# Reordering steps in a two-layer transformer kernel on one core: four-bit lines, key split, normalised rows, second normalisation

## Chip, core and metric

One NeuronCore of one Trainium2 chip runs the whole program in one launch. The metric is the device time of that launch in microseconds (us); lower is better. Engines are named as the profile names them: PE (TensorE, matrix products and transposes), ACT (ScalarE), DVE (VectorE), POOL (GpSimd), SP (the queue that issues the DMAs).

## The reference, cut to what matters

Four sequences of 256 tokens, width 512, pass through two pre-normalised layers. Each layer is an attention and a feed-forward part, both added to the residual stream.

```python
x = L0_attn_q                                   # (4, 256, 512) float32
x = x + attn0(layernorm(x))    # 32 heads in 8 groups, causal, softmax, output projection
x = x + lora(layernorm(x))     # 64 experts of rank 16, the 16 best by score, softmax gates
x = x + attn1(layernorm(x))    # q and k RMS-normalised, ALiBi slopes, softmax, projection
x = x + ffn(layernorm(x))      # gate, up and down weights in four-bit NF4 codes x absmax
```

A four-bit weight is `NF4_CODE[q] * absmax` of its block of 64. It has to be unpacked before it is multiplied.

## The kernel before

**Precision.** Every product is float32 made of three fp32r products: each operand is split into a high and a low part, and a matmul is `lo*hi + hi*lo + hi*hi` (lines 312 to 314). So each operand has a split: on the way out of PSUM the high part is an ACT copy (`pt_hi`, `ot_hi`, `qt_hi`, `kt_hi`, `xt_hi`) and the low part a DVE subtraction (`pt_lo`, `ot_lo`, `qt_lo`, `kt_lo`, `xt_lo`). Weights that come by DMA, and the second layer's keys, are split by POOL (`split_steps`, lines 570 and 571).

**Slots.** An attention layer walks over 8 groups of heads, and in each over 4 batches. One pair (group g, batch b) is a slot. Seven turns of a hardware loop hold slots b = 1, 2, 3 of group g and slot 0 of group g+1 (`slot_steps`); before them stand lead steps and a first slot, behind them the last three slots of the last group (`last_slot_steps`) and a tail (`tail_steps`). What a slot does is written out as one list of steps. PE, ACT, DVE, POOL and SP each walk the same list in order, each issuing only its own share of a step and waiting on semaphores for the others. Where a step stands in the list therefore sets its place in every engine's queue.

The steps of a slot that matter here:

- `pt_split`: three transposed probability tiles of the slot before leave PSUM, `pt_hi` on ACT (L804), `pt_lo` on DVE (L862).
- `scores`, `mask`, `max`, `exp`, `normalise`: the softmax of this slot. PE makes the scores; DVE masks, takes the maximum and its bias; ACT takes the exponential (L813); DVE divides (L900). Part 0 are the first 128 queries, part 1 the second 128 with all 256 keys.
- `tile`: one of six 512-wide projections (K, Q0 to Q3, V) for a half of the tokens, made ahead for later slots. The main results go alternately to two PSUM banks (`ring`); a bank is free again when DVE has taken the low part out of it.
- `pv`: probabilities times values on PE, then `ot_hi` (ACT) and `ot_lo` (DVE). PE waits here for all three `pt_lo`.
- `out`: the output projection of 128 tokens, added to x by DVE (L911).
- `transpose`: the normalised probabilities, part 0 (L784), then part 1 (L791).
- `dq_lines` (ACT, four or eight ACTIVATE, L546), `dq_top` (DVE, L553 and L555) and `dq_value` (POOL, L561, L562, then `centre` L537 for the next codes): one tile of four-bit weights unpacked in each slot of the first attention, written to HBM for the last part. `dq_lines` waits until `centre` is done.
- second layer only: `q_rms`, `k_rms`, `roots` and `k_norm`. In `k_norm` PE spreads the key's root (L777), DVE multiplies the keys by it (L967), and POOL copies and splits them (L1019, L570, L571); the scores of the slot after need that split. `w_next` is the refill of one weight tile: SP loads it and POOL splits it (2 instructions).

**The layer norm.** `norm_stats` (DVE) takes mean and variance of a batch of x, `norm_root` takes the inverse root (14 small instructions on POOL, or on DVE), `norm_write` writes the normed rows into `xn` (ACT, L473, or DVE, L419) and `norm_turn` transposes them (PE, L460) and splits them into `xt_hi` and `xt_lo`. `xn` holds one batch, so the next write has to wait for the transposes of the last. ACT's `norm_write` also waits until DVE has freed every ring tile that ACT has counted up to there. In the last slots a batch is normed as soon as its x is complete, so that the next part can begin.

**Around the attentions.** Behind the first attention stand the experts, which begin with the scores of batch 0. Behind the second stands the four-bit part. It works in units of one 512-wide gate and up product (`unit`), `silu`, `h`, then `down`; its first list of steps is `opening`, and `lines`, `top`, `value` there are the unpacking of the `late` weights.

Of the kernel before, what the change touches and what calls it, by code (L numbers as in the profile page):

```python
# [34 lines left out]
GROUPS, HEADS = 8, 4  # L35
# [11 lines left out]
K, Q0, Q1, Q2, Q3, V = range(6)  # L47
# [50 lines left out]
def slot_steps(b, rms):  # L98


    if rms:
        half, ahead = (0 if b in (1, 2) else 1), (0 if b == 0 else 1)
        tiles = [K, Q0, Q1] if b in (1, 3) else [Q2, Q3, V]
    else:
        half, ahead = (1, 0) if b in (0, 1) else (0, 1)
        tiles = [K, Q0, Q1] if b in (0, 2) else [Q2, Q3, V]
    t = [("tile", x, half, ahead) for x in tiles]
    roots = rms and b in (1, 3)
    s = [("pt_split",)] + ([] if rms or b == 1 else [("dq_lines", 0)])
    s += [("scores", 0), ("mask", 0), ("max", 0, 0)]  # L110
    s += t[0:1] + [("max", 1, 0)] if rms else [("max", 1, 0)] + t[0:1]
    s += [("exp", 0), ("normalise", 0)] + t[1:2]
    s += [] if rms else [("exp", 1)]
    s += [("q_rms_turn", 1 if b == 1 else 0)] if roots else []
    s += [("pv",)] + ([("exp", 1)] if rms else [("dq_lines", 0)] if b == 1 else [])
    s += [("roots", 1 if b == 1 else 0)] if roots else []
    s += [("k_rms", half)] if rms and tiles[0] == K else []
    s += [("roots_done",)] if roots else []
    s += t[2:3] + [("normalise", 1)] + ([] if rms else [("dq_lines", 1), ("dq_top", 0)]) + [("out", 0)]
    s += [("v_turn", half)] if tiles[-1] == V else []  # L120
    s += [("w_next", X) for X in (Q0, Q1)] if rms and b == 3 else []
    s += [("k_norm", 1 if b == 1 else 0)] if roots else []
    s += [] if rms else [("dq_top", 1)]
    if rms:
        s += [("out", 1), ("q_rms", half, 0 if tiles[0] == K else 1)]
    else:
        s += [("out", 1), ("dq_value",)] if b == 0 else [("dq_value",), ("out", 1)]
    return s + [("transpose",)]


def first_slot_steps(rms):


    softmax = [[("scores", 0), ("mask", 0), ("max", 0, 0)], [("max", 1, 0), ("exp", 0), ("normalise", 0)], [("exp", 1)]]
    if rms:
        s = [("q_rms", 1, 0), ("tile", Q2, 1, 0)] + softmax[0] + [("w_next", K)] + softmax[1] + [("tile", Q3, 1, 0)]
        s += [("w_next", Q0)] + softmax[2] + [("tile", V, 1, 0), ("q_rms", 1, 1), ("w_next", Q1), ("v_turn", 1)]
        return s + [("normalise", 1)] + [("w_next", X) for X in (Q2, Q3, V)] + [("transpose",)]
    s = softmax[0] + [("tile", K, 1, 0)] + softmax[1] + [("tile", Q0, 1, 0)] + softmax[2] + [("tile", Q1, 1, 0)]
    return s + [("normalise", 1), ("dq_first",), ("transpose",)]  # L140


def last_slot_steps(b, rms):


    if b == 1 and not rms:
        return [step for step in slot_steps(1, rms) if step[0][0:3] != "dq_"][:-1] + [("scores", 1), ("transpose",)]
    s = [("pt_split",)] + ([("norm_turn", 0)] if b == 3 else []) + ([("scores", 0)] if b == 1 else [])
    if rms and b == 1:
        s += [("q_rms_turn", 1), ("pv",), ("mask", 0)]  # L150
    else:
        s += [("mask", 0), ("pv",)]
    s += [("max", 0, 0), ("exp", 0), ("max", 1, 0)] + ([("roots", 1)] if rms and b == 1 else [])
    s += norm_begin([b - 2], "pool") if b >= 2 else []
    s += [("normalise", 0), ("exp", 1), ("normalise", 1), ("out", 0)]
    s += [("k_norm", 1)] if rms and b == 1 else []
    if rms and b in (1, 2):
        s += [("ffn_hi", k) for k in (2 * b - 2, 2 * b - 1)] + [("ffn_lo", k) for k in (2 * b - 2, 2 * b - 1)]
    s += [("norm_write", b - 2, "act")] if b >= 2 else []
    s += [("out", 1)] + ([("scores", 1)] if b < 3 else [])  # L160
    return s + [("transpose",)]


def norm_begin(batches, who):


    s = [("norm_stats", batches), ("norm_root", batches, who)]
    return s + ([("norm_write", batches[0], "dve")] if who == "dve" else [])
# [15 lines left out]
    return s + [("tile", x, 0, 0) for x in (Q1, Q2, Q3, V)] + [("v_turn", 0)]  # L184


def tail_steps():

    return [("pt_split",), ("norm_turn", 1), ("pv",)] + norm_begin([2], "pool") + [("norm_write", 2, "act"), ("out", 0), ("out", 1),
                                                                 ("norm_turn", 2)]  # L190


RING_STEPS = ("tile", "k_rms", "v_turn", "q_rms", "q_rms_turn", "k_norm", "out")
# [51 lines left out]
def build(nc, x_in, w_attn, w_dense, lora_a, lora_wr, lora_b, norm_w, codes, absmax, kept, out):  # L245

    with ExitStack() as ctx:
# [3 lines left out]
        def sb(name, shape, dt=F32, scope=ctx):  # L251
            return scope.enter_context(nc.sbuf_tensor(name, shape, dt))
# [322 lines left out]
        def attention(layer, scope):  # L575
            rms = layer == 1
# [484 lines left out]
            def walk(eng, do, grows, pool_like=False):  # L1061


                xn_lead[0] = p1[:, :, :].rearrange("p h k -> p (h k)").rearrange("p (t d) -> p t d", d=D) if rms else None
                do(eng, lead_steps(rms), 0, None)
                xn_lead[0] = None
                lead2[0] = True
                do(eng, first_slot_steps(rms), 0, 0)
                lead2[0] = False
                last = GROUPS - 1  # L1070

                def turn(g, **more):
                    for b in (1, 2, 3):
                        do(eng, slot_steps(b, rms), g, b, **more)
                    do(eng, slot_steps(0, rms), g + 1, 0, **more)

                if pool_like:
                    turn_loop(eng, last - 1, grows, turn)
                    turn(last - 1, refill=not rms, final=True)
                else:  # L1080
                    turn_loop(eng, last, grows, turn)
                if do is pe_steps:
                    last_slots[layer] = pe_ring.n
                for b in (1, 2, 3):
                    do(eng, last_slot_steps(b, rms), last, b)
                do(eng, tail_steps(), GROUPS, 0)


            hi_turn = 2 * (WT - 1 - rms) + 2
# [404 lines left out]
        def nf4(scope):  # L1494
# [3 lines left out]
            h_hi = sb("h_hi", [P, 2, TOK], F32R, scope)  # L1498
            h_lo = sb("h_lo", [P, 2, TOK], F32R, scope)
# [10 lines left out]
            def tops(par, ahead):  # L1510
                return [("top", par, 0, ahead), ("top", par, 1, ahead), ("value", par, ahead)]
# [19 lines left out]
                return s + half_unit(3) + (splits(1, 2, 3) if more else []) + downs(more)  # L1531

            opening = [("centre", 0, 0), ("centre", 1, 0), ("unit", 0), ("lines", 0, 0, 0), ("lines", 0, 1, 0)]
            opening += norm_begin([3], "dve") + [("silu", 0), ("h", 0), ("h_hi", 0), ("norm_turn", 3), ("h_lo", 0)]
            opening += tops(0, 0) + [("unit", 1), ("lines", 1, 0, 0), ("silu", 1), ("top", 1, 0, 0), ("h", 1)]
            opening += [("h_hi", 1), ("lines", 1, 1, 0), ("h_lo", 1), ("top", 1, 1, 0), ("value", 1, 0)]
            opening += half_unit(2) + splits(0, 4, 5) + splits(1, 0, 1) + half_unit(3) + splits(1, 2, 3) + downs(True)
# [183 lines left out]
        with d_scope:  # L1721
            pe_d, act_d, dve_d, pool_d, sp_d = nf4(d_scope)
# [135 lines left out]
```

## Time and profile before

| | |
|---|---|
| median of 3 runs | 1869.03 us (1868.91 to 1872.07) |
| profiled execution | 1863.55 us |
| its span | 1861.8 us |
| PE busy | 1751.9 us, 94% |
| DVE busy | 1296.9 us, 70% |
| ACT busy | 877.7 us, 47% |
| POOL busy | 788.6 us, 42% |
| granted TensorE clock, mean | 0.981 |

The profiled execution is one run; its span is first instruction to last. The engines work side by side, so PE's 94% says that the other 110 us are the time in which PE waited. A busy figure alone does not say which wait can be removed; for that the waits of PE are read in their place. The parts lie in the span like this: first attention to about 710 us, experts to 840, second attention to 1610, four-bit part to the end. A turn of the first attention's loop takes some 84 us, one of the second some 90.

### The profile page before, as it was taken

How to read it: one execution, taken by the hardware profiler on the slowest of the kernel's cores; microseconds unless marked ns; L12 is line 12 of the kernel's file. 1: busy time of each engine (PE TensorE's matmuls, PEld its weight loads, DVE VectorE, ACT ScalarE, POOL GpSimd, SP SyncE). 2: the span in 40 equal slices, each digit the busy share in tenths (PEclk: the TensorE clock that was granted, in tenths of full speed). 3: DMA queues.
4: the chain of work that ended last, by engine and by line, in shares of the span. 5: the costliest groups of instructions: out<-in, count | busy, mean ns of one | idle time of the engine just before them, and what ended most of it. 6: DMA issues, size and time to landing. Idle time of an engine off the chain costs nothing.

```text
span 1861.8 us, 28756 instructions
## 1 busy us (share of the span) xinstructions
PE 1751.9 (94%) x8864; PEld 1449.6 (78%) x8864; DVE 1296.9 (70%) x2317; ACT 877.7 (47%) x2288; POOL 788.6 (42%) x924
## 2 busy tenths in 40 slices
PE   8999999999999977997899999999999997889999
PEld 7787878788787866885778787878787886668887
DVE  5787778777788765345677777877777776655555
ACT  3556565556555634222444444444444444454543
POOL 5334425262534433144545454545454424244442
PEclk9999999999999998999899999999999999999999
DMA  4022122121112121000101000000001002022121
GB/s 143 33 68 73 60 64 90 43 95 65 62 62 77 47 71 57 1 7 23 35 29 28 28 29 28 28 28 28 28 28 28 23 0 80 0 69 68 56 56 46
DMA packets 47711, 87.77 MB, mean 47 GB/s; under 512 B 6576, under 2 KB 6576, under 8 KB 47536
## 3 DMA queue, kind: packets, MB, share of 16 engines
q1 hardware_dynamic: 47664, 87.19, 14.8%
q8 instruction: 24, 0.39, 0.1%
q14 instruction: 23, 0.19, 0.0%
HBM read 77.73 MB, written 9.44 MB: 47 GB/s over the span
## 4 chain that ended last, share of the span: by engine, by line
PE 54%; DVE 6%; POOL 4%; ACT 3%; issue 2%; POOLq 0%; DVEq 0%; ACTq 0%
PE ring L312 10%; PE ring L314 9%; PE ring L313 9%; PE scores L312 3%; PE scores L314 3%; PE scores L313 3%; PE turned L312 3%; PE turned L313 3%; PE turned L314 3%; PE scores L705 2%; PE turned L791 1%; PE turned L755 1%; PE turned L756 1%; PE turned L777 1%; PE turned L784 1%
## 5 line engine op out<-in xcount | busy, mean ns | idle before, releaser
L312 PE MATMUL ring<-xt_hi,w_lo 128*128 128x512 f32 x768 | 306.3, 399 | 18.9 <-DVE kt_lo L930 14.9
L313 PE MATMUL ring<-xt_lo,w_hi 128*128 128x512 f32 x768 | 304.7, 397 | 0.0
L314 PE MATMUL ring<-xt_hi,w_hi 128*128 128x512 f32 x768 | 304.5, 397 | 0.0
L312 PE MATMUL ring<-wd_hi,ot_lo 128*128 128x512 f32 x512 | 208.3, 407 | 8.2 <-DVE ot_lo L906 6.4
L804 ACT CAST pt_hi<-turned 128x512 fp32r<-128x512 f32 x192 | 100.6, 590 | 237.7 <-PE turned L784 231.0
L313 PE MATMUL ring<-wd_lo,ot_hi 128*128 128x512 f32 x512 | 203.7, 398 | 0.0
L314 PE MATMUL ring<-wd_hi,ot_hi 128*128 128x512 f32 x512 | 203.6, 398 | 0.0
L312 PEld LDWEIGHTS ring<-xt_hi,w_lo 128*128 128x128 f32 x768 | 145.6, 190 | 53.9 <-issue 19.1
L570 POOL TENSOR_SCALAR sq_hi<-sq 128x512 fp32r<-128x512 f32 x80 | 55.0, 687 | 305.4 <-ACT sq L830 286.9
L314 PEld LDWEIGHTS ring<-xt_hi,w_hi 128*128 128x128 f32 x768 | 145.3, 189 | 34.9
L546 ACT ACTIVATE lv_early<-code_early 128x512 f32<-128x512 f32 x224 | 122.6, 631 | 102.9 <-POOL code_early L537 95.0
L313 PEld LDWEIGHTS ring<-xt_lo,w_hi 128*128 128x128 f32 x768 | 145.7, 190 | 31.4
L900 DVE TENSOR_TENSOR p<-p,rsum 128x512 f32<-128x512 f32 (+1 forms) x128 | 150.1, 1173 | 4.4
L862 DVE TENSOR_TENSOR pt_lo<-turned,pt_hi 128x512 fp32r<-128x512 f32 x192 | 120.8, 683 | 35.9 <-ACT pt_hi L804 35.9
L830 ACT ACTIVATE sq<-ring 128x512 f32<-128x512 f32 x80 | 48.3, 604 | 191.6 <-PE ring L314 183.5
L813 ACT ACTIVATE p<-scores,bias,root 128x128 f32<-128x128 f32 (+1 forms) x256 | 128.0, 519 | 19.0 <-DVE bias L890 19.0
L561 POOL TENSOR_TENSOR deq_early<-lv_early 128x512 f32<-128x512 f32 x28 | 37.9, 1354 | 228.8 <-DVE lv_early L555 196.9
L571 POOL TENSOR_TENSOR w_lo<-w_raw,w_hi 128x512 fp32r<-128x512 f32 x96 | 130.2, 1356 | 8.0
L930 DVE TENSOR_TENSOR qt_lo<-ring,qt_hi 128x512 fp32r<-128x512 f32 x128 | 88.1, 688 | 61.7 <-ACT qt_hi L840 60.3
L911 DVE TENSOR_TENSOR x<-x,ring 128x512 f32<-128x512 f32 x128 | 87.0, 682 | 53.4 <-PE ring L314 52.8
L570 POOL TENSOR_SCALAR w_hi<-w_raw 128x512 fp32r<-128x512 f32 x96 | 77.0, 802 | 110.9 <-DMA w_raw<-w_attn_dram 57.4
L906 DVE TENSOR_TENSOR ot_lo<-turned,ot_hi 128x512 fp32r<-128x512 f32 x128 | 83.5, 685 | 57.7 <-ACT ot_hi L819 57.6
(247 smaller groups left out, 4480.6 us busy)
## 6 DMA issues: line engine op xcount, KB each, us to landing
w_raw<-w_attn_dram SPq DMA_DIRECT2D x96, 256.0 KB, 3.1
wd_raw<-w_dense_dram SPq DMA_DIRECT2D x64, 256.0 KB, 2.7
code_early<-codes_dram SPq DMA_DIRECT2D x28, 256.0 KB, 2.8
absmax_early<-absmax_dram SPq DMA_DIRECT2D x56, 128.0 KB, 3.0
kept_dram<-deq_early SPq DMA_DIRECT2D x28, 256.0 KB, 2.0
stage<-kept_dram SPq DMA_DIRECT2D x28, 256.0 KB, 2.7
code_late<-codes_dram SPq DMA_DIRECT2D x14, 256.0 KB, 2.7
absmax_late<-absmax_dram SPq DMA_DIRECT2D x28, 128.0 KB, 2.9
```

Of the source, the lines that this page charges most:

```text
L312: nc.tensor.matmul(o, l_lo, r_hi, start=start, stop=False)
L313: nc.tensor.matmul(o, l_hi, r_lo, start=False, stop=False)
L314: return nc.tensor.matmul(o, l_hi, r_hi, start=False, stop=stop)
L546: ins = nc.scalar.activation(lv[:, q, :], code[:, par, :], ACT.Copy, bias=offset, scale=scale)
L570: pool_link(nc.gpsimd.tensor_scalar(dst_hi, src, 1.0, 0.0, ALU.mult, ALU.add))
L571: nc.gpsimd.tensor_tensor(dst_lo, src, as_f32(dst_hi), ALU.subtract).then_inc(sem_done, 1)
L804: nc.scalar.copy(pt_hi[:, j, :, :], turned[:, j, :, :]).then_inc(s_pt_hi, 1)
L813: ins = nc.scalar.activation(pr[:, h, :], sc[:, h, :], ACT.Exp, bias=bias[:, k, h:h + 1], scale=scale, accum_out=sums[:, k, h:h + 1])
L862: nc.vector.tensor_tensor(pt_lo[:, j, :, :], turned[:, j, :, :], as_f32(pt_hi[:, j, :, :]), ALU.subtract).then_inc(s_pt_lo, 1)
L900: nc.vector.tensor_tensor(pr[:, :, :], pr[:, :, :], rsum[:, k, :].unsqueeze(2).to_broadcast([P, HEADS, width]), ALU.mult).then_inc(s_prob, 1)
L911: dve_ring_free(nc.vector.tensor_tensor(x[:, t, :], x[:, t, :], tile, ALU.add))
L930: dve_ring_free(nc.vector.tensor_tensor(lo, tile, as_f32(hi), ALU.subtract))
```

## The change

It moves steps in the lists and removes no work.

1. Third slot (b = 2) of the first attention: `dq_lines 0` (4 ACTIVATE) moves from behind `pt_split` to behind `pv`, where the second slot has it already.
2. Fourth slot (b = 3) of the second attention: `k_norm` moves ahead of the refills of Q0 and Q1.
3. First slots. First attention: `exp 0` and `exp 1` come ahead of Q0's tile step, `max 1` ahead of K's, and `normalise 1` ahead of Q1's. Second: `normalise 1` moves ahead of `q_rms`.
4. Last slots and tail: the `norm_write` of a batch moves from its slot's end to behind the next slot's `pt_split`, and its `norm_turn` from ahead of `pv` to behind it. In the second slot of the second attention `k_norm` moves behind the second `out`.
5. The last attention's tail leaves `norm_turn 2` to the four-bit part, where it stands behind the first unit and the root of batch 3.

```diff
@@ slot_steps
-    s = [("pt_split",)] + ([] if rms or b == 1 else [("dq_lines", 0)])
+    s = [("pt_split",)] + ([] if rms or b in (1, 2) else [("dq_lines", 0)])
...
-    s += [("pv",)] + ([("exp", 1)] if rms else [("dq_lines", 0)] if b == 1 else [])
+    s += [("pv",)] + ([("exp", 1)] if rms else [("dq_lines", 0)] if b in (1, 2) else [])
...
+    s += [("k_norm", 1 if b == 1 else 0)] if roots else []
     s += [("w_next", X) for X in (Q0, Q1)] if rms and b == 3 else []
-    s += [("k_norm", 1 if b == 1 else 0)] if roots else []
@@ first_slot_steps
-        s += [("w_next", Q0)] + softmax[2] + [("tile", V, 1, 0), ("q_rms", 1, 1), ("w_next", Q1), ("v_turn", 1)]
-        return s + [("normalise", 1)] + [("w_next", X) for X in (Q2, Q3, V)] + [("transpose",)]
-    s = softmax[0] + [("tile", K, 1, 0)] + softmax[1] + [("tile", Q0, 1, 0)] + softmax[2] + [("tile", Q1, 1, 0)]
-    return s + [("normalise", 1), ("dq_first",), ("transpose",)]
+        s += [("w_next", Q0)] + softmax[2] + [("tile", V, 1, 0), ("normalise", 1), ("q_rms", 1, 1), ("w_next", Q1)]
+        return s + [("v_turn", 1)] + [("w_next", X) for X in (Q2, Q3, V)] + [("transpose",)]
+    s = softmax[0] + softmax[1][0:1] + [("tile", K, 1, 0)] + softmax[1][1:] + softmax[2] + [("tile", Q0, 1, 0)]
+    return s + [("normalise", 1), ("tile", Q1, 1, 0), ("dq_first",), ("transpose",)]
@@ last_slot_steps
-    s = [("pt_split",)] + ([("norm_turn", 0)] if b == 3 else []) + ([("scores", 0)] if b == 1 else [])
+    s = [("pt_split",)] + ([("norm_write", 0, "act")] if b == 3 else []) + ([("scores", 0)] if b == 1 else [])
...
-        s += [("mask", 0), ("pv",)]
+        s += [("mask", 0), ("pv",)] + ([("norm_turn", 0)] if b == 3 else [])
...
-    s += [("k_norm", 1)] if rms and b == 1 else []
     if rms and b in (1, 2):
         s += [("ffn_hi", k) for k in (2 * b - 2, 2 * b - 1)] + [("ffn_lo", k) for k in (2 * b - 2, 2 * b - 1)]
-    s += [("norm_write", b - 2, "act")] if b >= 2 else []
-    s += [("out", 1)] + ([("scores", 1)] if b < 3 else [])
+    s += [("out", 1)] + ([("k_norm", 1)] if rms and b == 1 else []) + ([("scores", 1)] if b < 3 else [])
@@ tail_steps
-    return [("pt_split",), ("norm_turn", 1), ("pv",)] + norm_begin([2], "pool") + [("norm_write", 2, "act"), ("out", 0), ("out", 1),
-                                                                 ("norm_turn", 2)]
+    s = [("pt_split",), ("norm_write", 1, "act"), ("pv",), ("norm_turn", 1)] + norm_begin([2], "pool")
+    s += [("out", 0), ("out", 1), ("norm_write", 2, "act")]
+    return s + ([] if rms else [("norm_turn", 2)])
@@ nf4, opening
-            opening += norm_begin([3], "dve") + [("silu", 0), ("h", 0), ("h_hi", 0), ("norm_turn", 3), ("h_lo", 0)]
+            opening += [("norm_stats", [3]), ("norm_root", [3], "dve"), ("norm_turn", 2), ("norm_write", 3, "dve")]
+            opening += [("silu", 0), ("h", 0), ("h_hi", 0), ("norm_turn", 3), ("h_lo", 0)]
```

## Rows read from the trace of the kernel before

**Rows 1.** The page: PE's line, and PE's clock in 40 slices (tenths).

```profile
PE 1751.9 (94%) x8864; PEld 1449.6 (78%) x8864; DVE 1296.9 (70%) x2317; ACT 877.7 (47%) x2288; POOL 788.6 (42%) x924
...
PEclk9999999999999998999899999999999999999999
```

**Rows 2.** Waits of PE: us in total, times, longest us.

```profile
PE ring L312 <- DVE kt_lo L930: 14.9, 6, 2.7
PE ring L460 <- ACT xn L473: 14.9, 7, 3.5
PE scores L705 <- POOL kt_lo L571: 10.7, 7, 1.7
```

**Rows 3.** Windows: three third slots; length, busy of PE, PEld, DVE, ACT, POOL, clock.

```profile
74.13:93.85 19.72, 19.72 (x103) 16.47 (x101) 15.88 (x26) 12.41 (x35) 3.22 (x3) 1.00 0.12 41
153.73:177.86 24.13, 20.18 (x103) 16.38 (x101) 16.65 (x25) 12.31 (x35) 9.72 (x9) 1.00 0.12 36
237.75:261.69 23.94, 21.62 (x102) 17.54 (x101) 17.16 (x25) 12.41 (x35) 9.54 (x9) 0.93 0.13 39
```

**Rows 4.** Timeline of the second of these: start, us, engine, [idle before, releaser].

```profile
163.90 2.19 ACT L546 ACTIVATE lv_early<-code_early 128x512 f32<-128x512 f32 x4 [7.97 <-POOL code_early L537]
167.68 0.49 PE L312 MATMUL ring<-xt_hi,w_lo 128*128 128x512 f32 x1 [2.52 <-DVE kt_lo L930]
172.17 0.48 PE L312 MATMUL ring<-wd_hi,ot_lo 128*128 128x512 f32 x1 [1.43 <-DVE ot_lo L906]
```

**Rows 5.** Timeline of a fourth slot's end, second attention.

```profile
1058.08 1.87 DVE L900 TENSOR_TENSOR p<-p,rsum 128x1024 f32<-128x1024 f32 x1
1058.84 1.59 POOL L570 TENSOR_SCALAR w_hi<-w_raw 128x512 fp32r<-128x512 f32 x1
1060.47 0.67 DVE L967 TENSOR_TENSOR k_raw<-k_raw,turned 128x512 f32<-128x512 f32 x1
1063.73 0.40 POOL L1019 TENSOR_SCALAR kt_f<-k_raw 128x256 f32<-128x256 f32 x1
1066.12 1.16 PE L705 MATMUL scores<-kt_f,qt_f 128*128 128x128 f32 x8 [1.71 <-POOL kt_lo L571]
```

**Rows 6.** Timelines of the two first slots.

```profile
49.20 0.69 DVE L930 TENSOR_TENSOR qt_lo<-ring,qt_hi 128x512 fp32r<-128x512 f32 x1 [1.78 <-ACT qt_hi L840]
51.56 1.75 PE L791 MATMUL turned<-ident,p 128*128 128x128 f32 x7 [2.86 <-DVE p L900]
904.69 1.54 PE L791 MATMUL turned<-ident,p 128*128 128x128 f32 x6 [2.49 <-DVE p L900]
```

**Rows 7.** Timeline of the first attention's last slots and tail.

```profile
663.11 0.50 PE L312 MATMUL turned<-pt_hi,v_lo 128*128 128x512 f32 x1 [1.72 <-DVE pt_lo L862]
676.26 1.52 ACT L473 ACTIVATE xn<-x,shift,rstd 128x512 f32<-128x512 f32 x2 [5.28 <-POOL shift L448]
677.21 1.33 PE L460 MATMUL ring<-ident,xn 128*128 128x128 f32 x8 [2.10 <-ACT xn L473]
680.22 0.80 PE L312 MATMUL turned<-pt_hi,v_lo 128*128 128x512 f32 x1 [1.67 <-DVE pt_lo L862]
715.11 0.45 PE L312 MATMUL ring<-xt_hi,a_lo 128*64 128x256 f32 x1 [2.34 <-DVE xt_lo L490]
```

**Rows 8.** Timeline from the second attention's last slots to the four-bit part.

```profile
1551.63 1.13 PE L777 MATMUL turned<-ident,root 128*128 128x128 f32 x8 [4.08 <-DVE q_slope L960]
1557.62 1.13 PE L705 MATMUL scores<-kt_f,qt_f 128*128 128x128 f32 x8 [0.52 <-POOL kt_lo L571]
1634.25 0.50 PE L312 MATMUL scores<-xt_hi,w_lo 128*128 128x512 f32 x1 [3.78 <-DVE hf L1655]
```

**Rows 9.** Windows: three stretches in the last slots; columns as in rows 3.

```profile
678.80:685.70 6.90, 5.48 (x13) 4.34 (x14) 5.07 (x10) 2.56 (x5) 0.00 (x0) 0.51 0.00 0
695.90:702.80 6.90, 5.57 (x17) 4.43 (x18) 3.77 (x6) 3.83 (x8) 0.00 (x0) 0.51 0.00 0
1552.70:1556.10 3.40, 3.40 (x10) 2.62 (x9) 2.27 (x3) 0.04 (x1) 0.97 (x2) 0.50 0.00 0
```

More of the change, by code:

```diff
@@ L184, in lead_steps, with tail_steps @@
     return s + [("tile", x, 0, 0) for x in (Q1, Q2, Q3, V)] + [("v_turn", 0)]
-def tail_steps():
-    return [("pt_split",), ("norm_turn", 1), ("pv",)] + norm_begin([2], "pool") + [("norm_write", 2, "act"), ("out", 0), ("out", 1),
-                                                                 ("norm_turn", 2)]
+def tail_steps(rms):
+    s = [("pt_split",), ("norm_write", 1, "act"), ("pv",), ("norm_turn", 1)] + norm_begin([2], "pool")
+    s += [("out", 0), ("out", 1), ("norm_write", 2, "act")]
+    return s + ([] if rms else [("norm_turn", 2)])
 RING_STEPS = ("tile", "k_rms", "v_turn", "q_rms", "q_rms_turn", "k_norm", "out")
@@ L1085, in walk @@
                     do(eng, last_slot_steps(b, rms), last, b)
-                do(eng, tail_steps(), GROUPS, 0)
+                do(eng, tail_steps(rms), GROUPS, 0)
             hi_turn = 2 * (WT - 1 - rms) + 2
```

## The prediction

> **What bounds the kernel now.** I read the page first: PE is busy for 1751.9 of the 1861.8 us, so 110 us are waits of PE, and the clock line has dips to 0.8 and 0.9 [rows 1]. No other engine is near that share, so the time is PE's work, plus its waits, plus what a low clock adds. Next I read PE's waits in total [rows 2], then each wait's place on the timeline. The reader is to see that they are few and regular. The kt_lo wait comes in six of the seven third slots of the first attention's loop. The kt_lo wait of POOL is once per turn of the second loop in six turns, 1.7 each, and once at 1557.62 with 0.52 [rows 2, 8]. Of the seven xn waits three stand in each attention's last slots and tail (14.2 us together) and one in the experts. Last I read the windows for the clock, because a wait can be followed by a stretch at 0.50, which is 1.2 of the 2.4 GHz [rows 9].
>
> **Part 1, the four-bit lines in the third slot.** The lines of the third slot wait for POOL's `centre`, which here is done 10.2 us after the slot begins. ACT stands idle for 7.97 us with the copies of K, both exponentials and ot_hi queued behind it. So kt_lo is late and PE waits 2.52 us for its bank, and then 1.43 us for ot_lo [rows 4]. In the first turn `centre` is early, nothing waits, and the slot takes 19.72 us of PE work. In the turn after it takes 24.13, and in the next 23.94, with one wait and a clock of 0.93 instead of the second wait [rows 3]. So a late `centre` costs 4.2 to 4.4 us per turn, whether as wait or as clock.
> Behind `pv` the 4 ACTIVATE come when ACT has made both exponentials and ot_hi. K is ready some 6.5 us into the slot as in the first turn, and by the durations of this slot (two copies, exp 0, two copies, exp 1, two ot_hi) ACT reaches the lines some 13 us in, about 3 us after `centre` is done; that chain of POOL hangs on the output weights of an earlier slot and not on this slot's pace. The lines take 2.19 [rows 4] and then stand ahead of Q1's copies, which end 1.5 us after Q1 is ready; normalise 1 follows at some 18 us, and the transposes need it at 20. So the slot should fall to 19.7 to 20.1. The tops and the x adds end 2 to 3 us behind the transposes, as they do in the first turn, and their next reader is a pv four tiles later. Bounds: the kt_lo waits alone go (6 x 2.5 = 15), or all to the floor (6 x 4.35 = 26). I take 24.5.
>
> **Part 2, key split ahead of two refills.** DVE's multiply of the keys ends at 1061.14, POOL is then in the refills and begins the key's copies at 1063.73; they last 2.3 us, and PE, idle since 1064.41, starts the scores at 1066.12 [rows 5]. With the split first it runs 1061.2 to 1063.5, 0.9 us before PE wants it. The whole 1.71 goes in six turns: 10.2. The two refills, some 4 us, come 2.4 us later; POOL's next work is the squares of the slot after, 8 us behind, and SP's loads that wait for these refills are wanted more than 10 us later. If the split were held up by another 1.9 us (the length of the longest DVE instruction near it, L900), 1.0 of each wait would stay and the part were worth 4.2; that is the lower bound.
> The rows show such a hold: the refill's first instruction took 1.59 beside a 1.87 us DVE instruction with two SBUF inputs [rows 5]. The Trainium skill (SBUF — State Buffer, Who interferes with whom) says that a DVE instruction with two SBUF inputs contends with a GpSimd instruction that reads SBUF, and that the later one fully blocks. By that rule the split's new neighbours (adds with one input from PSUM) do not hold it and the part is worth 10.2; if any DVE neighbour did, it would be 4.2. The trace cannot yet say which, since no row has the split there.
>
> **Part 3, the first slots.** In the first attention DVE waits 1.78 us for ACT's qt_hi before Q1's subtraction, and normalise 1 is queued behind it; PE waits 2.86 for that [rows 6]. Now normalise 1 stands behind Q0's subtraction instead. The exponentials come 1.3 us earlier but Q0's copies now stand between, so I get normalise 1 some 1.2 us earlier, and the clock may stay up (up to 3.4 more): 1.2 to 4.6, I take 2.5. In the second, normalise 1 waits behind q_rms and v_turn though its exponentials are done 5 us before; PE's 2.49 [rows 6] goes but v_turn comes 0.5 later: 2.0 to 3.7, I take 2.5. Sum 5, bounds 3 and 8.
>
> **Part 4, last slots and tail.** Transposes end at 675.11 (677.21 less 2.10). ACT then waits for POOL's root until 676.26 and writes two xn (1.52) before it copies pt_hi, so pv starts at 680.22. In the slot before, with nothing in between, pv waits 1.72 behind the transposes [rows 7]. So after the change it starts at 675.11 + 1.72 = 676.83, 3.4 earlier. norm_turn (1.33) now comes behind pv, and its two xt_lo delay the maxima by 1.3: the next transposes come 3.3 earlier, not more. In the tail the same happens, longer, since POOL's root ends later there; pv comes some 4.4 earlier again. The root of batch 2 and its turn follow pv as before, so that wait stays, and so does 2.34 for the experts' first product [rows 7]. Together 7.8, of which some 4.8 is work that the old slots did at a clock of 0.51 [rows 9]; if one such stretch remains it is 1 to 2 less. Bounds 3 and 8.5, I take 7.
> In the second attention the same two turns give 2.4 and 3.4, and norm_turn 2 behind the first unit takes its xn wait off PE; but the four-bit part then goes by ACT and DVE (lines, xt_hi, write 3, h), which the wait of 3.78 at 1634.25 shows [rows 8]. Following that chain, it comes 6.3 earlier in all.
> Against this stands `k_norm` behind the second out. PE's wait of 4.08 for the roots [rows 8] is partly filled by the out (3.0 us), but the scores behind hang on roots, key multiply and POOL's split, and DVE's multiply now follows one more add of 0.7. They start 0.6 later, at 1558.2, and PE idles 5.7 us before them with 1 us of small work. After 4.08 idle the clock was 0.50 for 3.4 us [rows 9]; after more idle I expect the same under the scores, half of 3.4 = 1.7. With another dip elsewhere in these slots (1.0), the second attention's end gives 6.3 - 0.6 - 1.7 - 1.0 = 3.0, bounds -2 and 6.
>
> **The sum.** 24.5 + 10.2 + 5 + 7 + 3.0 = 49.7 us off the profiled execution's 1863.55 (span 1861.8): 1813.9. That execution is 5.5 us under the median of the runs shown, 1869.03; the gain is the same from there, so I predict 1819.3. The bounds give 15 + 4.2 + 3 + 3 - 2 = 23 and 26 + 10.2 + 8 + 8.5 + 6 = 59: 1846 and 1810, and 5.5 less if the runs should fall where the profiled one did.
>
> **Rivals.**
> A. *The third slot gives back half.* ACT or DVE becomes the slot's bound: lines, Q1's copies, normalise 1 and the tops all queue at its end. DVE is busy for 16.65 of 24.13 [rows 3], which would be 84% of a slot of 19.8. For it: the order there has only 2 us of slack. Against: the second slot has this order already and runs without a wait. Part 1 is 12 and the time 1832.
> B. *The ends give nothing.* Waits only change their names: pv waits for pt_lo, the scores for the kt split, and the clock stays low. For it: every one of those chains is longer than PE's work there. Then 10 less: 1829.
> C. *Slower.* `centre` in the third slot slips past the point where ACT gets to the lines. From 3 us later than now it stops ACT ahead of Q1's copies and the second lines, and every further us is one us in each of six turns. To eat 49.7 us it must come 3 + 8.3 = 11 us later than now: say 12, which gives 1874. Against: POOL does the same work in the same order, and `centre` has stood at the same place in the turns that I read.
> D. *It does not do what it says.* Waits of PE are replaced one for one because PE's own queue was not waiting for what the profile names: 1869.
>
> **How the numbers follow.** My forecast 0.74, A 0.11, B 0.09, C 0.03, D 0.03. The range 1806 to 1838 takes in the forecast with its bounds, A and B, and leaves out C and D and the far ends. A change of 0.2% (3.7 us) is about what a measurement of this kernel tells from none. Faster by more than that: 0.94 (forecast, A, B). Within it: D, 0.03. Slower: C, 0.03.
>
> **What the changed profile would show.** Part 1: no kt_lo wait at L312, ACT's idle time before lv_early gone from the third slots, and these slots at 19.7 to 20.1; a wait of L784 for p or of L312 for qt_lo in them speaks for A. Part 2: no wait of L705 in the second loop, and the key split ahead of two w splits. Part 3: L791's waits at 1.7 and near 0. Part 4: two xn waits fewer in the first attention; pt_lo waits of 1.7 to 2.2 in their place; the first unit some 10 us earlier but its second half only 6; and a wait of some 5 us of L705 behind the second out of the second attention's last group, then a clock of 0.50. I should be wrong above all if the slots shorten and new waits of the same size show on ot_lo or p in the slot behind.

## The result, and the profile after

The changed kernel takes 1815.65 us (median of 4 runs, 1813.52 to 1816.80) against 1868.97 for the kernel before (1867.81 to 1872.07). The ratio is 0.9711, with a 95% interval of 0.9694 to 0.9728: 53 us or 2.9% faster. Forecast were 1819.3 us. The profiled execution took 1815.49 us with a span of 1813.8.

The page: PE's line and its clock in 40 slices. They answer to [rows 1].

```profile
PE 1739.9 (96%) x8864; PEld 1445.1 (80%) x8864; DVE 1299.4 (72%) x2317; ACT 877.6 (48%) x2288; POOL 786.2 (43%) x924
...
PEclk9999999999999998999999999999999999999999
```

No work has gone: each engine has as many instructions in this line as before. PE's busy time is 12 us less and its idle time fell from 110 to 74 us; together that is the 48 us. The mean granted clock rose from 0.981 to 0.986; an estimate from the two means (the missing share times the span, 35 and 25 us) puts some 10 of the 12 us down to it. (The lines of the changed kernel stand one lower than before: L312 is L311 here.)

PE's waits, in total. They answer to [rows 2].

```profile
PE turned L311 <- DVE pt_lo L861: 10.7, 6, 1.9
PE ring L311 <- DVE xt_lo L489: 9.2, 8, 2.3
PE scores L704 <- POOL kt_lo L570: 6.4, 1, 6.4
PE turned L754 <- POOL sq_lo L570: 5.4, 2, 2.9
```

The six kt_lo waits of DVE are gone from the list. POOL's kt_lo was waited for seven times with 10.7 us, and is now waited for once, but for 6.4. The waits for xt_lo are partly new: the turned rows stand behind pv and the output product behind them.

Windows of the changed kernel: the third slots of the first two turns, then the fourth slot behind the second of them. Columns as in [rows 3].

```profile
69.81:89.47 19.66, 19.66 (x102) 16.52 (x101) 15.02 (x24) 12.42 (x35) 3.22 (x3) 1.00 0.12 41
149.86:169.51 19.65, 19.65 (x102) 16.52 (x101) 15.30 (x23) 12.43 (x35) 10.07 (x9) 1.00 0.15 47
169.51:190.13 20.62, 20.33 (x106) 16.86 (x105) 17.44 (x28) 12.25 (x34) 3.22 (x3) 1.00 0.11 38
```

The second third slot took 24.13 [rows 3] and now takes as long as that of the first turn. The fourth slot has 0.29 of idle time in it. It is part of a price of 0.5 that the slot behind pays (20.62 against 20.11 before), and experiment 5 takes it away. ACT's first instructions on the four-bit lines of that slot, in the kernel before and in the changed one:

```profile
182.48 2.19 ACT L546 ACTIVATE lv_early<-code_early 128x512 f32<-128x512 f32 x4 [2.42 <-POOL code_early L537]
...
175.74 2.20 ACT L545 ACTIVATE lv_early<-code_early 128x512 f32<-128x512 f32 x4 [4.02 <-POOL code_early L536]
```

The slot begins at 177.86 and 169.51: ACT gets to the lines 4.6 us into it before and 6.2 now, and Q2's copies and the exponentials stand behind.

Timeline of that third slot in the changed kernel, to be read against [rows 4].

```profile
156.49 0.37 ACT L834 COPY kt_f<-ring 128x256 f32<-128x256 f32 x1 [4.42 <-PE ring L313]
...
159.40 0.94 POOL L536 TENSOR_SCALAR code_early<-code_early 128x512 f32<-128x512 int32 x1
...
162.79 2.25 ACT L545 ACTIVATE lv_early<-code_early 128x512 f32<-128x512 f32 x4
```

`centre` is as late in the slot as before (10.5 us in), but K's copies no longer wait for it, and ACT comes to the lines 2.45 us after it is done. The forecast had "about 3". `centre` itself took 0.94 us here instead of 0.62; it ran beside DVE's `normalise`, which took 0.86 instead of 0.69.

Timeline of a fourth slot's end in the second attention, against [rows 5].

```profile
1025.86 0.67 DVE L966 TENSOR_TENSOR k_raw<-k_raw,turned 128x512 f32<-128x512 f32 x1
...
1026.69 0.41 POOL L1018 TENSOR_SCALAR kt_f<-k_raw 128x256 f32<-128x256 f32 x1 [2.44 <-DVE k_raw L966]
...
1027.77 1.28 POOL L570 TENSOR_TENSOR kt_lo<-k_raw,kt_hi 128x512 fp32r<-128x512 f32 x1
...
1029.02 0.61 POOL L569 TENSOR_SCALAR w_hi<-w_raw 128x512 fp32r<-128x512 f32 x1
...
1029.64 1.06 PE L704 MATMUL scores<-kt_f,qt_f 128*128 128x128 f32 x8
```

The split now ends at 1029.05, 0.6 before PE wants it, the scores have no wait, and the refills follow. The split takes 2.36 us from its first copy to its end, against 2.33 before: nothing held it.

Where the 48.1 us between the two profiled spans came from can be read off matching transposes (the first of each slot) in both traces. The first slot of the first attention is 4.7 shorter, the loop and the slots up to the third of the last group 22.9, the last slots up to the experts' first product 8.7 (715.11 [rows 7] against 679.20). Then 6.8 are lost again up to the first transposes of the second attention. That slot is 3.6 shorter, the loop 11.6, and the way from the last group to the end gives 3.7; the start differs by 0.4. The sum is 4.7 + 22.9 + 8.7 - 6.8 + 3.6 + 11.6 + 3.7 - 0.4 = 48.0.

Of the 6.8 us lost, 0.7 belong to part 3. `normalise 1` now stands ahead of `q_rms` on DVE, so `v_turn`, just ahead of those transposes, comes later; PE waits 1.49 for it here and 0.77 with the old order. Timelines of the changed kernel and of undo_first (experiment 3):

```profile
871.09 1.11 PE L736 MATMUL turned<-ident,vt 128*128 128x128 f32 x4 [1.49 <-DVE xn L942]
...
869.62 1.11 PE L736 MATMUL turned<-ident,vt 128*128 128x128 f32 x4 [0.77 <-DVE xn L942]
```

### The profile page after: what moved, and what is told of

Same layout as the page of the kernel before. It is cut to its first block, busy times and chain, and to the rows that moved or that the text cites. A ratio compares the mean times of both kernels' runs of the same rounds, so it can differ in the third digit from the quotient of the medians.

```text
span 1813.8 us, 28744 instructions
## 1 busy us (share of the span) xinstructions
PE 1739.9 (96%) x8864; PEld 1445.1 (80%) x8864; DVE 1299.4 (72%) x2317; ACT 877.6 (48%) x2288; POOL 786.2 (43%) x924
## 4 chain that ended last, share of the span: by engine, by line
PE 55%; DVE 5%; ACT 3%; POOL 2%; issue 2%; DMA 0%; POOLq 0%; DVEq 0%; ACTq 0%; SPq 0%
PE ring L311 10%; PE ring L312 10%; PE ring L313 10%; PE scores L311 3%; PE scores L313 3%; PE scores L312 3%; PE turned L311 3%; PE turned L313 3%; PE turned L312 3%; PE scores L704 2%; PE turned L790 2%; PE turned L783 1%; PE turned L754 1%; PE turned L776 1%; PE turned L755 1%
## 5 line engine op out<-in xcount | busy, mean ns | idle before, releaser
L311 PE MATMUL ring<-xt_hi,w_lo 128*128 128x512 f32 x768 | 304.6, 397 | 3.9 <-DVE qt_lo L929 1.5
L312 PE MATMUL ring<-xt_lo,w_hi 128*128 128x512 f32 x768 | 303.8, 396 | 0.0
L311 PE MATMUL ring<-wd_hi,ot_lo 128*128 128x512 f32 x512 | 207.6, 405 | 9.8 <-DVE xt_lo L489 5.0
L312 PE MATMUL ring<-wd_lo,ot_hi 128*128 128x512 f32 x512 | 202.8, 396 | 0.0
L311 PEld LDWEIGHTS ring<-xt_hi,w_lo 128*128 128x128 f32 x768 | 145.1, 189 | 36.6 <-DVE qt_lo L929 2.0
L312 PEld LDWEIGHTS ring<-xt_lo,w_hi 128*128 128x128 f32 x768 | 144.9, 189 | 31.5
L899 DVE TENSOR_TENSOR p<-p,rsum 128x512 f32<-128x512 f32 (+1 forms) x128 | 154.2, 1205 | 4.4
L311 PEld LDWEIGHTS ring<-wd_hi,ot_lo 128*128 128x128 f32 x512 | 96.4, 188 | 36.2 <-issue 8.9
L887 DVE TENSOR_REDUCE negmax<-scores 128x4 f32<-128x512 f32 (+1 forms) x128 | 121.9, 953 | 2.1
```

Source lines behind the costliest of these rows:

```text
L311: nc.tensor.matmul(o, l_lo, r_hi, start=start, stop=False)
L312: nc.tensor.matmul(o, l_hi, r_lo, start=False, stop=False)
L887: dve_link(nc.vector.tensor_reduce(negmax[:, k, :], sc[:, :, :], AX.X, ALU.max, negate=True))
L899: nc.vector.tensor_tensor(pr[:, :, :], pr[:, :, :], rsum[:, k, :].unsqueeze(2).to_broadcast([P, HEADS, width]), ALU.mult).then_inc(s_prob, 1)
```

## Experiments

Each run was compared with the kernel before on the same chip (medians there 1869.4 to 1870.0). The differences in us below are taken from the changed kernel's 1815.65, which is of an earlier set of runs. Measured again beside key_back, lines_fourth and both, the changed kernel took 1812.88 (after_again). So a difference of 3 us or less between medians tells nothing by itself; there the traces decide, stage by stage.

| run | median us | ratio, 95% interval |
|---|---|---|
| undo_lines | 1837.86 | 0.9835 (0.9814 to 0.9856) |
| undo_key | 1826.35 | 0.9768 (0.9743 to 0.9792) |
| undo_first | 1825.17 | 0.9766 (0.9746 to 0.9787) |
| undo_rows | 1831.08 | 0.9798 (0.9775 to 0.9821) |
| key_back | 1811.87 | 0.9696 (0.9674 to 0.9718) |
| lines_fourth | 1811.48 | 0.9687 (0.9673 to 0.9700) |
| both | 1806.90 | 0.9678 (0.9656 to 0.9700) |
| after_again | 1812.88 | 0.9703 (0.9688 to 0.9718) |
| undo_turn2 | 1816.55 | 0.9731 (0.9706 to 0.9756) |
| late_centre1 | 1815.67 | 0.9723 (0.9703 to 0.9742) |
| late_centre4 | 1835.60 | 0.9831 (0.9812 to 0.9851) |

**1. undo_lines: part 1 undone.**

```diff
-    s = [("pt_split",)] + ([] if rms or b in (1, 2) else [("dq_lines", 0)])
+    s = [("pt_split",)] + ([] if rms or b == 1 else [("dq_lines", 0)])
-    s += ... [("dq_lines", 0)] if b in (1, 2) else [])
+    s += ... [("dq_lines", 0)] if b == 1 else [])
```

> The changed kernel with its first part undone: the four-bit lines of the third slot stand behind pt_split again. My theory: ACT waits for POOL's centre ahead of K's copies again, so the kt_lo waits of 2 to 2.7 us come back in six third slots. In the two traces so far these slots differ by 26.4 us, and 3.5 come back from the fourth slots, which are 0.5 longer in the changed kernel: the run should take 23 us more than the changed kernel, 1838.5, and its fourth slots should be 0.5 shorter. Rival: the third slot gained from what stands around it (a faster turn of POOL or DVE), and the lines alone are worth half or less: 1827 or under, with the waits back but elsewhere made good.

Measured: 1837.86, 22.2 more than the changed kernel's median. PE's waits in total, first line:

```profile
PE ring L311 <- DVE kt_lo L929: 14.8, 6, 2.7
```

The six waits are back with their old size (14.9 [rows 2]). The six third slots are 4.2 to 4.7 us longer, 26 in all, and the seven fourth slots 0.5 shorter. The theory holds; the rival asked for 1827 or less.

**2. undo_key: part 2 undone.**

```diff
-    s += [("k_norm", 1 if b == 1 else 0)] if roots else []
     s += [("w_next", X) for X in (Q0, Q1)] if rms and b == 3 else []
+    s += [("k_norm", 1 if b == 1 else 0)] if roots else []
```

> The changed kernel with its second part undone: k_norm stands behind the refills of Q0 and Q1 again. My theory: the wait of the scores for POOL's kt_lo, 1.7 us, comes back in six turns, and with it the restart that makes a turn 1.97 shorter in the changed trace: 11.6 us more, 1827. Rival: the split was held by DVE instructions with two SBUF inputs and its place hardly counts: 4 us more, 1820.

Measured: 1826.35, 10.7 more. The wait is back in six turns, which with the one of 6.4 makes 16.7:

```profile
PE scores L704 <- POOL kt_lo L570: 16.7, 7, 6.4
```

In the trace a turn is 1.98 us longer in five of the six and 3.5 in one, where a stretch at a clock of 0.50 came upon it.

**3. undo_first: part 3 undone.** Both first slots stand in the order before, as in the diff ahead of the prediction.

> The changed kernel with its third part undone: the first slots of both attentions in the old order. My theory: waits of 2.9 and 2.5 us for p come back, each with a stretch at a clock of 0.50: 4.7 and 3.6 by the two traces, 8 in all, 1824. Rival: the clock does not depend on these waits, and only the waits' own 1.9 and 2.5 come back: 4 us, 1820.

Measured: 1825.17, 9.5 more. Timeline of the first attention's first slot in this run:

```profile
51.68 1.97 PE L790 MATMUL turned<-ident,p 128*128 128x128 f32 x8 [2.86 <-DVE p L899]
```

Its window behind that wait (length, busy of PE, PEld, DVE, ACT, POOL, clock, DMA):

```profile
50.90:57.70 6.80, 6.02 (x28) 6.02 (x29) 2.71 (x4) 1.17 (x2) 1.20 (x1) 0.50 0.16 41
```

The same place in the changed kernel:

```profile
50.09 1.09 PE L790 MATMUL turned<-ident,p 128*128 128x128 f32 x8 [0.97 <-DVE p L899]
```

With the wait of 2.86 the clock falls to 0.50 and the eight transposes take 1.97; with one of 0.97 it stays up and they take 1.09. The slot's 4.7 us are 1.9 of wait; the other 2.8 are put down to the clock, as what is left. The second attention's first slot is 3.6 longer in this run, of which the 0.7 us of `v_turn` ahead of it are to be taken off. Both halves speak for the theory and against the rival.

**4. undo_rows: parts 4 and 5 undone, k_norm left behind the second out.** `norm_write` at the slot's end, `norm_turn` ahead of `pv`, the four-bit part's opening as before.

> The changed kernel with its fourth and fifth part undone but for k_norm, which stays behind the second out: xn is written ahead of the slot's end and turned ahead of pv, in both attentions, and the four-bit part opens as before. My theory: three xn waits come back in each attention's end; 8.7 us in the first attention and 7.2 in the second by the two traces (2.5 + 4.7), 16 in all, 1831.5. Rival: the pt_lo waits stand in for them and the gain of the ends is clock and chance: 8 us or less, 1823.

Measured: 1831.08, 15.4 more. The waits for xn are back (16.1, 7 times) and those for xt_lo fall from 9.2 to 4.1:

```profile
PE ring L459 <- ACT xn L472: 16.1, 7, 3.5
...
PE ring L311 <- DVE xt_lo L489: 4.1, 4, 2.3
```

So a part of the xn waits does live on under another name, but the ends give 15 us and not 8. The traces agree: from the first attention's third slot of the last group to the experts' first product 41.4 us pass instead of 32.8, and from the last group of the second attention to the end 329.2 instead of 321.9, 15.9 in all.

**5. lines_fourth: the lines behind pv in the fourth slot too.** This tests why that slot became longer.

```diff
-    s = [("pt_split",)] + ([] if rms or b in (1, 2) else [("dq_lines", 0)])
+    s = [("pt_split",)] + ([] if rms or b in (1, 2, 3) else [("dq_lines", 0)])
-    s += ... [("dq_lines", 0)] if b in (1, 2) else [])
+    s += ... [("dq_lines", 0)] if b in (1, 2, 3) else [])
```

> The changed kernel with the four-bit lines behind pv in the fourth slot too. My theory: the fourth slot is 0.5 us longer in the changed kernel because its centre is now later than the slot's pt_split, ACT waits for it and ot_hi, ot_lo and the output product come late by as much; with the lines behind pv that goes: 7 x 0.5 = 3.5 us less, 1812.1. Rival: the lines then delay the tops and x adds, and slot 0 of the next group pays the same: 1815.6 or more.

Measured: 1811.48, 4.2 under the changed kernel's first median and 1.4 under its second (1812.88). The window of that fourth slot, where the changed kernel needs 20.62:

```profile
169.07:189.18 20.11, 20.11 (x106) 16.96 (x105) 17.51 (x28) 12.23 (x34) 3.22 (x3) 1.00 0.12 39
```

All seven fourth slots are 0.5 shorter, to the length before, and slot 0 behind them is no longer. In the traces that is 3.5 us. The theory holds by the traces; the medians alone could not tell it from the rival.

**6. key_back: k_norm ahead of the second out again, in the last group's second slot of the second attention.**

```diff
     s += [("normalise", 0), ("exp", 1), ("normalise", 1), ("out", 0)]
+    s += [("k_norm", 1)] if rms and b == 1 else []
...
-    s += [("out", 1)] + ([("k_norm", 1)] if rms and b == 1 else []) + ([("scores", 1)] if b < 3 else [])
+    s += [("out", 1)] + ([("scores", 1)] if b < 3 else [])
```

> The changed kernel, but in the second slot of the second attention's last group k_norm stands ahead of the second out again, as before the change. My theory: that step of part 4 loses time, since the scores behind hang on roots, key multiply and POOL's split and not on PE. The wait of 6.4 us for kt_lo with its low clock goes back to 0.5, and the slot is 3.4 shorter: 1812.2. Rival: PE's wait of 4 us for the roots comes back and costs as much: 1815.6.

Measured: 1811.87, which is 3.8 under the first median of the changed kernel and 1.0 under its second. Timeline of this run, PE's wait for the roots:

```profile
1507.05 2.04 PE L777 MATMUL turned<-ident,root 128*128 128x128 f32 x8 [3.93 <-DVE q_slope L960]
```

Timeline of the changed kernel, the same step and the scores behind:

```profile
1507.32 1.13 PE L776 MATMUL turned<-ident,root 128*128 128x128 f32 x8 [1.26 <-DVE q_slope L959]
1514.82 2.05 PE L704 MATMUL scores<-kt_f,qt_f 128*128 128x128 f32 x8 [6.38 <-POOL kt_lo L570]
```

The window of the low clock in the changed kernel:

```profile
1512.20:1519.00 6.80, 4.18 (x19) 4.21 (x20) 0.00 (x0) 0.00 (x0) 2.25 (x3) 0.50 0.15 39
```

With k_norm in front the wait for the roots is 3.9 and the scores have none; behind, it is 1.3 but the scores wait 6.4 and run at a clock of 0.50 (2.05 us for the eight that take 1.05 in key_back). This run has a stretch of 6.8 us at 0.50 too, but from 1505.4, under the roots and the second out, where the key's chain is still under way: the scores start 21.6 us into the slot with it, 21.4 before the change and 22.9 in the changed kernel. From transposes to transposes this slot takes 23.8 to 23.9 us in the three traces with k_norm in front (before, key_back, both) and 27.2 to 27.3 in the ten with it behind. The difference is 3.3 to 3.5 us for every pair, so this step of the change costs time, though the medians of this run do not show it.

**7. both: experiments 5 and 6 together.**

> The two edits before together: k_norm ahead of the second out, and the lines behind pv in the fourth slot too. My theory: they stand in different places and add up, 6.9 us less than the changed kernel, 1808.7. Rival: each gives half: 1812.5.

Measured: 1806.90, 8.8 under the changed kernel's first median, 6.0 under its second, and the lowest median of all versions. Its five runs spread from 1803.70 to 1814.43, and its interval overlaps with those of the two single edits and of after_again, so the runs alone do not prove that it beats them. In the trace both effects stand whole: fourth slots 0.5 shorter seven times, and the last group's slot 3.4 shorter.

**8. after_again: the changed kernel once more.** It asks about the 6.8 us lost ahead of the second attention (all but the 0.7 of `v_turn`).

> The changed kernel itself once more, for the stretches at a clock of 0.50 that its trace has in the experts and in the second attention's lead steps (four stretches, about 6.8 us lost against the trace of before, at waits that both kernels have). My theory: where a wait of PE of 1.4 to 2.9 us falls decides whether the clock drops behind it, and that differs from execution to execution; the waits will stand at the same places and some of the four stretches will be gone or moved, with a time of 1813 to 1818. Rival: the same waits always bring the same stretches, as a cost of the change: the four stand at the same instructions again.

Measured: 1812.88, just under the range expected. The window 800 to 880 of the changed kernel:

```profile
800.00:880.00 80.00, 64.62 (x290) 50.92 (x290) 42.39 (x86) 22.84 (x54) 41.47 (x47) 0.91 0.12 34
```

The same window of this second execution:

```profile
800.00:880.00 80.00, 64.63 (x304) 50.85 (x303) 46.60 (x94) 25.63 (x65) 43.10 (x46) 0.96 0.12 37
```

The same program shows a clock of 0.91 in one execution and 0.96 in the other, and from the first attention's last transposes to the second's first it takes 5.1 us less. The four stretches of the first trace (from 734, 765, 809 and 826) are gone, so the rival falls: the same waits do not always bring them.

Whether the change makes them more frequent is not shown. From the experts' first product to the second attention's first transposes three of the twelve traces with changed lists (after_again, undo_first, both) take 186.0 to 187.1 us and nine take 189.6 to 192.8. Of the kernel before there is one trace, with 186.0.

Nor does every stretch follow a long wait, as the theory had it. Ahead of the one at 733.9 the longest idle time of PE is 0.23 us. Two windows of the changed kernel, ahead of the stretch and in it:

```profile
730.50:733.90 3.40, 3.17 (x22) 2.62 (x22) 2.66 (x5) 1.41 (x3) 1.12 (x1) 1.00 0.00 0
733.90:737.40 3.50, 3.50 (x19) 3.50 (x18) 3.33 (x16) 1.67 (x4) 3.50 (x4) 0.51 0.00 0
```

One wait shows by itself that it does not fix the clock behind it. In the changed kernel's trace:

```profile
826.39 0.76 PE L754 MATMUL turned<-sq_lo,pick 128*128 128x512 f32 x1 [2.55 <-POOL sq_lo L570]
```

and the window behind it:

```profile
826.10:829.50 3.40, 3.11 (x7) 2.48 (x8) 0.74 (x2) 0.00 (x0) 0.15 (x1) 0.50 0.02 5
```

The same wait in the second execution:

```profile
822.40 0.47 PE L754 MATMUL turned<-sq_lo,pick 128*128 128x512 f32 x1 [2.54 <-POOL sq_lo L570]
```

and the window around it:

```profile
815.00:840.00 25.00, 18.30 (x84) 14.23 (x84) 9.64 (x17) 6.22 (x13) 7.22 (x8) 1.00 0.00 1
```

The wait is as long, the clock is not. All 13 traces have this wait, with 2.54 or 2.55 us. Behind it the clock falls in five (the changed kernel, undo_lines, undo_rows, late_centre1, late_centre4) and stays up in eight.

**9. undo_turn2: part 5 alone undone.**

```diff
-    return s + ([] if rms else [("norm_turn", 2)])
+    return s + [("norm_turn", 2)]
-            opening += [("norm_stats", [3]), ("norm_root", [3], "dve"), ("norm_turn", 2), ("norm_write", 3, "dve")]
+            opening += norm_begin([3], "dve")
```

> The changed kernel with its fifth part alone undone: norm_turn 2 stands in the second attention's tail again, ahead of the four-bit part's first unit, and batch 3 is normed as before. My theory: the four-bit part's opening goes by ACT and DVE (write 2, eight lines, silu, h), and by the old trace and by the new one 9.7 us pass from write 2 to h_hi in either order. PE gets its xn wait of 2 to 3 us back ahead of the first unit but loses less later: 0 to 1 us more than the changed kernel, 1816. Rival: PE bounds the opening and the whole wait comes back: 3 to 4 us more, 1819.

Measured: 1816.55, 0.9 more, within what the intervals can tell from none; late_centre1, measured on the same chip and as fast as the changed kernel, had 1815.67. From the last group's last transposes to the first down product the two traces take 49.9 and 49.4. Timeline of ACT in this run:

```profile
1560.38 1.52 ACT L472 ACTIVATE xn<-x,shift,rstd 128x512 f32<-128x512 f32 x2 [7.08 <-POOL shift L447]
...
1570.13 0.62 ACT L1615 CAST h_hi<-hf 128x512 fp32r<-128x512 f32 x1 [0.75 <-DVE hf L1655]
```

The same two in the changed kernel:

```profile
1562.46 1.52 ACT L472 ACTIVATE xn<-x,shift,rstd 128x512 f32<-128x512 f32 x2 [7.08 <-POOL shift L447]
...
1571.77 0.62 ACT L1615 CAST h_hi<-hf 128x512 fp32r<-128x512 f32 x1 [0.75 <-DVE hf L1655]
```

From the write of batch 2 to h_hi 9.75 us pass in the one and 9.31 in the other, so the expectation had the new trace wrong (9.75 is also what the kernel before takes). Moving `norm_turn 2` takes a wait of 1.78 off PE and shortens its wait for hf from 3.78 to 1.94, but adds one of 2.53 for batch 3's rows. It gives about half a microsecond up to the first down product. From the last transposes to the end the two traces differ by 1.0 (267.6 and 266.6), but traces that share the changed kernel's steps here differ by 0.7 among themselves.

**10. late_centre1 and late_centre4: centre made later.** One or four POOL subtractions whose result nobody reads stand ahead of the second slot's `centre` (the counter of POOL's chain grows with them).

```diff
+                        if b == 1:
+                            for _ in range(4):
+                                pool_link(nc.gpsimd.tensor_tensor(xn[:, 0, :], lv[:, 0, :], lv[:, 4, :], ALU.subtract))
                         if not (final and b == 0):
                             pool_centre(pool, 2 * g + b // 2 + 1, b % 2, code)
```

> The changed kernel with one more POOL subtraction of 512 columns (1.3 us, its result is not used) ahead of the second slot's centre in the loop of the first attention, so that the third slot's codes come 1.4 us later. My theory: ACT reaches the third slot's lines 2.45 us after centre is done, so nothing changes: 1815.7. Rival: POOL's chain or its reads beside DVE already count: 6 x 1.4 = 8 us more, 1824.

> The same with four such subtractions, so that the third slot's codes come 5.5 us later. My theory: that is 3 us past the point where ACT gets to the lines, so Q1's copies, the bank of the second out and normalise 1 come 3 us late and PE waits in six third slots: 18 us more, 1834. Rival: there is slack behind the lines too, and a third of it or less shows: 6 us or less, 1821.

Measured: 1815.67 and 1835.60. Timeline of the third slot in late_centre4:

```profile
159.12 5.75 POOL L1032 TENSOR_TENSOR xn<-lv_early 128x512 f32<-128x512 f32 x4
165.12 0.62 POOL L536 TENSOR_SCALAR code_early<-code_early 128x512 f32<-128x512 int32 x1 [0.25 <-POOL xn L1032]
165.77 2.19 ACT L545 ACTIVATE lv_early<-code_early 128x512 f32<-128x512 f32 x4 [2.78 <-POOL code_early L536]
...
169.48 0.62 PE L311 MATMUL ring<-wd_hi,ot_lo 128*128 128x512 f32 x1 [2.49 <-DVE qt_lo L929]
```

In late_centre1 `centre` ends 11.5 to 12.2 us into the slot, still ahead of ACT, and the third slots stay at 19.7 to 19.95. In late_centre4 it ends at 16.0, 5.5 later than in the changed kernel; ACT waits 2.78 for it and begins the lines 3.1 later, which is the 5.5 less the slack of 2.45. Q1's low part comes late, and the second out waits 2.49 for its bank. Two of the six third slots are 2.9 and 3.2 us longer than in the changed kernel, about the 3.1. In the other four a stretch at a clock of 0.50 comes with the wait, and they are 4.2 to 4.7 longer. Windows of one slot of each kind:

```profile
149.71:173.93 24.22, 21.73 (x103) 17.68 (x102) 18.10 (x25) 12.58 (x35) 15.21 (x13) 0.93 0.12 38
318.15:340.95 22.80, 19.92 (x103) 16.46 (x102) 15.31 (x23) 12.50 (x35) 15.35 (x13) 1.00 0.12 37
```

Some fourth slots win up to 0.5 back. The loop is 22.5 us longer in the trace and the median 19.9. So what exceeds the slack is paid in full, and more where the clock falls. Rival C's mechanism is real, from 2.45 us on where the forecast said 3, and the change does not reach it.

## Why the prediction was right, point by point

- **Part 1** was put at 24.5 and measured 22.9 in the trace and 22.2 by undo_lines. The third slots fall to 19.65 to 19.8, at the lower edge of "19.7 to 20.1", and give 26.4 together. The 0.5 us that each fourth slot pays was missing from the sum. The text had said that the tops end later and that their next reader is far; the reader that counts is POOL's `value` and `centre`, and through them the lines, exponentials and ot_hi of the fourth slot. Rival A had the tops queue at the slot's end, but looked for the price in the third slot itself and took half the gain for it. The prediction's last sentence named the right place, new waits on ot_lo in the slot behind; they took 3.5 us, about a seventh.
- **Part 2**, 10.2, measured 11.6 (10.7 by undo_key). Each wait of 1.71 brought about 0.26 more around it; 0.1 of it is the first scores, which took 1.16 and now take 1.06. The split beside DVE's adds took 2.36 us against 2.33 before, so nothing held it and the lower bound of 4.2 did not come true. The Trainium skill (SBUF — State Buffer, Who interferes with whom) says that a DVE instruction with at most one SBUF input does not contend with GpSimd. The trace agrees: those adds have one input from PSUM. No run put the split beside a DVE instruction with two SBUF inputs.
- **Part 3**, 5, measured 8.3 in the trace, 7.6 with the 0.7 of `v_turn` taken off, and 9.5 by undo_first's median. The first slot was undersized, at 2.5 with an upper bound of 4.6, and gave 4.7: `normalise 1` came earlier than forecast, so PE's wait fell to 0.97 and not to 1.7, and the low stretch is gone wholly. The second gave 3.6 less 0.7, so 2.9 against 2.5: the wait of 2.49 is gone, `v_turn` costs 0.7 where the forecast had 0.5, and the low stretch is 6.8 us instead of 10.2.
- **Part 4**, first attention: 7 forecast, 8.7 measured. pv was to come 3.4 earlier and in the tail 4.4 more, and the transposes of the last group's fourth slot come 3.6 earlier, the experts' first product another 5.0. No stretch of low clock remained in this trace. In after_again one of 3.4 us did, from 664.1, and this way took 33.8 us instead of 32.8; the forecast's allowance of 1 to 2 us for it was right in kind.
- **Part 4 and 5**, second attention: 3.0 forecast, 3.7 measured. The turns and the four-bit part gave 7.2 where 6.3 were forecast. `k_norm` behind the second out costs 3.4 (key_back) where I had 0.6 + 1.7 and another 1.0 for a dip that did not come. The wait was seen in its place with 5.7 (6.4 measured), but the scores start 1.5 us later and not 0.6; from there to the transposes 1.9 us more pass, close to the 1.7 put down for the low clock. The sum of 3.3 was right by offsetting errors.
- **The base.** From the profiled execution of before 49.7 were forecast and 48.1 measured, after a loss of 6.8 that no step foresaw. Of it 0.7 is `v_turn`; the other 6.1 are stretches of low clock that the same program did without in after_again. Without them the profile would have come out at 54, and the medians differ by 53.3. So the total is better met than its parts, and that is in part luck: part 3 and the ends were sized too low, part 1 a little too high, and low clock that nobody forecast made up for it in the profile.

## What to carry to other kernels

When queues run in program order, look for the instruction that waits for something late while work that PE needs is queued behind it. Here moving 4 ACTIVATE from ahead of K's copies and the exponentials gave 22 us, and a price of 3.5, already taken off, appeared one slot further on, through POOL. Where several engines take turns on one chain (roots, multiply, split, scores), fill PE's wait only if the chain itself does not get longer: PE's wait for the roots fell by 2.7 us, the scores' grew by 6.

A wait of PE has to be priced with the clock that may fall behind it, as a range and not as one number: late_centre4's waits of 2.5 to 3.0 us cost 2.9 to 4.7 us each. A stretch at 0.50 costs less where it lies over work that something else is waiting out, as in key_back. And compare clock windows of more than one execution of the same program before such a stretch is put down to a change, and before it is called chance.

## What the runs showed of the hardware that was not expected

The granted clock fell to 0.50 (1.2 of 2.4 GHz) at a wait of PE in one execution and not in another, with the same wait at the same instruction of the same program: the 2.55 us at 826.39 of the changed kernel against the 2.54 us at 822.40 of its second execution. In 13 traces the clock fell behind this wait in five. It also fell, at 733.9 of the changed kernel, after 3.4 us at full clock in which PE idled for no more than 0.23. Between the two executions of the changed kernel such stretches moved the second attention's beginning by 5.1 us. In the first slot the clock fell in both traces with a wait of 2.86 us (before, undo_first) and stayed up in the eleven with one of 0.95 to 0.97.
